# Another order of score, maximum and value-sum work inside a head group of a 32-head attention

## The reference, cut to what matters

```python
def attention_fwd(x, wq, wk, wv, wo, n_heads=32):      # x is layernormed, T=1024, C=512
    xq, xk, xv = (x @ w.T reshaped to [B, T, 32, 16] for w in (wq, wk, wv))
    xq, xk = rotary_pos_emb(xq), rotary_pos_emb(xk)
    scores = einsum('bqhd,bkhd->bhqk', xq, xk) * 16 ** -0.5
    scores = where(causal, scores, -1e30)
    probs = softmax(scores, axis=-1)
    return einsum('bhqk,bkhd->bqhd', probs, xv).reshape(B, T, C) @ wo.T
```

## Time and profile before

| what | value |
| --- | --- |
| runs | 1281.04, 1281.21, 1270.77 us (median 1281.04) |
| profiled execution | 1278.5 us, its span 1276.6 us |
| TensorE busy | 1186.2 us (93%) |
| VectorE busy | 869.9 us (68%) |
| ScalarE busy | 355.9 us (28%) |
| first and last score matmul of the loop (L1582) | 634.6 and 874.7 us |
| scores, x384 | mean of a 512-column one 382 ns |
| exponentials, x384 | mean of a 512-column one 604 ns |

### The profile page before, as it was taken

The page is one execution under the profiler, slowest core; times in us unless marked ns, Lnnn a source line. Parts: engine busy times, 40 slices in busy tenths (PEclk is TensorE's granted clock), DMA queues, the critical chain, the costliest instruction groups (busy, mean ns, idle before and its releaser), DMA issues.

```text
span 1276.6 us, 28155 instructions
## 1 busy us (share of the span) xinstructions
PE 1186.2 (93%) x9962; PEld 513.8 (40%) x9962; DVE 869.9 (68%) x2483; ACT 355.9 (28%) x746; POOL 139.2 (11%) x191
## 2 busy tenths in 40 slices
PE   6799988999999999899899999999979899999992
PEld 3478563433333333444344444433624233333330
DVE  5832675977777773688888888841459677777763
ACT  5434610000000002232176666674110000000010
POOL 2200011111101101352000000000110101111000
PEclk9899978999999999999999999999989999999996
DMA  9100333157724345429405331005751646615556
GB/s 360 46 1 1 153 135 127 51 194 265 266 67 139 112 147 189 165 78 232 90 12 90 57 56 27 2 2 205 318 187 35 256 142 203 202 52 188 187 181 243
DMA packets 63669, 174.33 MB, mean 137 GB/s; under 512 B 9886, under 2 KB 16628, under 8 KB 61352
## 3 DMA queue, kind: packets, MB, share of 16 engines
q1 hardware_dynamic: 55471, 150.60, 36.8%
q0 software_dynamic: 5760, 18.88, 4.3%
q10 hardware_dynamic: 2296, 3.05, 0.7%
HBM read 785.47 MB, written 22.03 MB: 633 GB/s over the span
## 4 chain that ended last, share of the span: by engine, by line
PE 77%; DVE 10%; DMA 4%; ACT 3%; issue 3%; SPq 1%; POOL 1%; POOLq 0%; ACTq 0%; DVEq 0%
PE PS L1096 30%; PE PS L1115 13%; PE PS L1595 6%; PE PS L1582 5%; PE PS L1558 5%; PE PS L817 3%; PE PS L801 2%; PE PS L1622 2%; PE PS L1129 1%; PE PS L1515 1%; PE PS L581 1%; ACT arena L1663 1%; PE PS L565 1%; DVE PS L1716 1%; PE PS L1585 1%
## 5 line engine op out<-in xcount | busy, mean ns | idle before, releaser
L1096 PE MATMUL PS<-arena 128*32 128x400 f32 x3456 | 399.1, 504 | 7.6 <-DMA HH<-in_w 3.7
L1096 PE MATMUL PS<-HH,arena 128*32 128x400 f32 x1152 | 398.5, 504 | 0.0
L1096 PEld LDWEIGHTS PS<-arena 128*32 128x32 f32 x3456 | 144.2, 111 | 256.0 <-issue 248.3
L1286 DVE STREAM_TRANSPOSE arena<-arena 32x192 f32<-32x192 f32 x576 | 211.4, 367 | 7.2
L1716 DVE CUSTOM_DVE_ANT_0 PS<-PS,U 128x128 f32<-128x128 f32 (+7 forms) x256 | 188.0, 783 | 21.3 <-PE PS L1558 20.5
L1115 PE MATMUL PS<-arena 128*32 128x512 f32 x1512 | 195.5, 600 | 4.0 <-DVE arena L1286 4.0
L1663 ACT ACTIVATE arena<-PS 128x512 f32<-128x512 f32 (+3 forms) x384 | 164.2, 495 | 69.2 <-PE PS L1585 48.8
L1264 DVE STREAM_TRANSPOSE arena<-arena 32x128 f32<-32x128 f32 x544 | 164.7, 303 | 16.6 <-DMA arena<-h_scratch,RT 8.7
L1169 ACT ACTIVATE arena<-PS 128x400 f32<-128x400 f32 x72 | 36.2, 503 | 436.5 <-PE PS L1096 436.5
L1270 DVE TENSOR_TENSOR arena<-arena,PS 128x400 f32<-128x400 f32 x72 | 41.0, 572 | 138.1 <-ACT arena L1169 138.1
L1096 PEld LDWEIGHTS PS<-HH,arena 128*32 128x32 f32 x1152 | 126.2, 111 | 0.0
(11 more groups left out here) (255 smaller groups left out, 1250.6 us busy)
## 6 DMA issues: line engine op xcount, KB each, us to landing
arena<-in_w SPq DMA_DIRECT2D x456, 800.0 KB
arena<-in_w2a SPq DMA_DIRECT2D x266, 768.0 KB
HH<-in_w SPq DMA_DIRECT2D x152, 800.0 KB
HH<-in_w2a SPq DMA_DIRECT2D x38, 768.0 KB
arena<-split_scratch SPq DMA_DIRECT2D x96, 128.0 KB, 6.4
arena<-y_scratch SPq DMA_DIRECT2D x24, 256.0 KB, 5.5
split_scratch<-arena SPq DMA_DIRECT2D x8, 768.0 KB, 4.5
arena<-in_w2b SPq DMA_DIRECT2D x72, 64.0 KB
```

The source lines that it names most:

```text
L1096: mm = eng.matmul(PS[SR * j:SR * j + SR, 2 * hf + m, 0:FH], XBT[:, u, c, SR * j:SR * j + SR], W13[j][:, c // 2, m, c % 2, hf * FH:(hf + 1) ...
L1286: tr = eng.transpose(ACT_T[SR * b:SR * b + SR, u, :, rows], src[:, :, SR * b:SR * b + SR])
```

## The change

The string of 98 letters is replaced by another of 98 with the same counts (48 e, 34 m, 12 a, 2 c, 2 t). No instruction, no buffer and no semaphore is added or taken away; the banks of the ring and the counts waited for are worked out from the list as before.

```diff
-        GROUP1 = ("emememeacmeetemeaemememeaemeemeaemeemeacemeteemam"
-                  "meemmemeameemeemmaeeeeammmeeemmemamemeeeamememeea")
+        GROUP1 = ("emememeeemecameeemateemmaememeemeeemacameeteememm"
+                  "aememmeaemeeememeemaaeemeememememmameemeeemaameem")
```

## The result

In 20 runs each the change takes 1268.69 us (median, 1262.45 to 1274.10) against 1276.62 us before (1268.05 to 1282.27). The ratio of the two is 0.9943, with a 95% interval of 0.9927 to 0.9960: 0.6% faster, some 7 us by the ratio (7.9 between the medians), clear of noise and under 1%. A second set of runs on another occasion gave 0.9960 (0.9942 to 0.9978). The forecast was 1273, with 1262 to 1280 as its range, out of a sum of -6.6 us.

The account below looks back on a forecast made before the run. TensorE was taken to bound the loop, with gain in the time it holds no work. Terms of -0.94 us a pass over seven passes gave -6.6 us, 1271.9 from the profiled 1278.5; forecast set at 1273, range 1262 to 1280.

Parts of the forecast that it names:

- wait A: Second turn: TensorE waits 0.36 us for the copy of bank 7; forecast to fall to 0.10, -0.26 a pass.
- wait T: First turn: TensorE waits 0.18 us for a copy; forecast to go, -0.18 us a pass.
- wait B: Fourth score after sum 8: 0.30 us until the first bank is back; forecast to go, -0.30 a pass.
- Step 1: Three pairs of sums (4-5, 8-9, 11-12) save 0.20 us each at their edges, -0.60 us a pass.
- Steps 2 to 4: Both turns and the fourth score after sum 8: wait A -0.26, wait T -0.18, wait B -0.30 us a pass.
- Step 5: Two runs of seven scores: new waits behind ScalarE's pace, 0.15 us each, +0.30 us a pass.
- Step 6: At `mtr`: its slack behind `shift` shrinks from 0.6 to about 0.1 us, +0.10 us a pass.
- Step 7: Pass 7, without maxima: cost of pairs against waits given back, taken as 0, bounds -0.5 and +1.1 us.
- TensorE is full anyway: Loop: waits move rather than go, only 0.35 us a pass to gain, 1276 to 1278 us; chance 0.24.
- All goes: Loop: waits of 0.84 and pairs of 0.69 us a pass all go, none new, 1268 us; chance 0.20.
- VectorE becomes the bound: At `mtr` and the scores behind it: TensorE waits for VectorE, slower than before, 1289 us; chance 0.05.
- The loop's gain does not reach the end: Behind the loop: the weights' traffic sets the end, 1278 to 1281 us; chance 0.03.

Follow-up runs that it names:

- t4_pair89: Kernel before with sum 8 moved behind the second of four masked scores and sum 9 ahead of the third; period 30.50 us against 30.78.
- t6_mtr: Kernel before with `mtr` moved one letter back, behind the first score after sum 9; period 31.22 us against 30.78.
- t2_middle: Kernel before with letters 21 to 50 taken from the change; period 30.31 us against 30.78, loop 235.8 us against 240.0.
- t3_last: Kernel before with letters 51 to 98 taken from the change; period 30.45 us against 30.78, loop 238.4 us against 240.0.
- t8_best: Another string with the change's counts and two pairs of sums, 4-5 and 8-9; period 29.22 us, ratio 0.9910 to the kernel before.
- t5_split: The change with its three pairs of sums taken apart; period 30.64 us against the change's 29.84, ratio 0.9983 to the kernel before.

## Why the prediction was right, term by term

The period fell by 0.94 as forecast, and the loop by 6.6. The mechanism was right: waits A, T and B went, and the pairs saved their edges. That the sum agrees to the hundredth is luck: one term of 0.2 was not seen, and several that came out better than forecast made up for it.

The measured column comes from the distances between the starts of TensorE's matmuls over one period of each kernel, less what the same two kinds of matmul take where nothing is waited for.

| step | forecast | measured |
| --- | --- | --- |
| 1, three pairs | -0.60 | -0.69 (each 0.09 on the way in, 0.12 on the way out, 0.02 in the second sum) |
| 1, not seen: `mtr` loses its neighbour | 0 | +0.21 |
| 2, wait A | -0.26 | -0.32 |
| 3, wait T | -0.18 | -0.15 |
| 4, wait B | -0.30 | -0.30 |
| 5, waits of scores, and of maxima for the ring | +0.30 | +0.29 |
| 6, `mtr` waits for `shift` | +0.10 | +0.03 |
| not placed, each under 0.03 | | -0.01 |
| sum | -0.94 | -0.94 |

- **Step 1** took the price of a sum's edge from the loop's last pair, and the Trainium skill's rule ("TensorEngine Tiling (Array Packing)", Key Properties: changing the tiling mode drains TensorE) for all widths. The rows gave 0.23 a pair and I took 0.20, thinking that a load runs ahead of its matmul; a sum's does so by 0.01 here (709.55 and 709.56), and 0.23 it is. The runs agree with the rule: the price is one of crossing between narrow and full, at every width. Whether the engine drains in that time they do not show. The rule should have been carried further. `mtr` puts its result in 12 partitions, and it behaves as a narrow one: it pays behind a mask and does not beside a sum. Before, it stood beside sum 9 and shared that sum's switches; the earlier trace rows showed both instructions, and I read them for the wait alone. The change moved two scores in between. t4_pair89 and t6_mtr show the 0.2.
- **Steps 2 to 4** were waits read between starts, and each went. Wait T left 0.03: the turn itself starts in time, and its second matmul comes 0.03 later than in the kernel before. Wait A left 0.04.
- **Step 5** was the right size, but the waits lie elsewhere as well. In the change they are 0.12 at score 6, 0.09 at score 31, 0.13 at score 40, 0.08 at score 46, 0.07 at maximum 32 and 0.04 and 0.03 at maxima 14 and 12, together 0.55; before there were 0.26 (0.13 and 0.04 at two scores, 0.06 and 0.03 at two maxima).
- **Step 6**: the slack at `mtr` went from 0.6 to about nothing, as worked out (0.1); the wait is 0.03.
- **Step 7**: pass 7 took 25.7 us before and 25.5 now, from its first score to its last; I had 0. Both sides that I had set against each other are there: in t2_middle it is 24.9 (wait A and the pair 4-5 gone), in t3_last 26.4 (the two other pairs). These 0.2 and the seven passes, which fell by 6.4 and not 6.6 because the first one gained only 0.7, make the 6.6 of the loop.
- **TensorE is full anyway** (0.24) is refuted: the loop's busy share left 0.35 us a pass, and 0.94 was taken out. It read 29.65 of 30 before and reads 30.00 now, with t8_best 0.6 us faster still. Matmul time in a row is no measure of room here.
- **All goes** (0.20) failed on the score runs and on `mtr`'s edge. t8_best, at -1.56 a period, shows that as much (1.53) was to be had, with another string.
- **VectorE becomes the bound** (0.05) did not come. t5_split and t6_mtr show how near it is: 0.2 us a pass each, at the ring. The share that I gave it (88%) divided the busy time of 30 us by a period of 29.8; over one period it is 27.0 of 29.84, 91%.
- **The loop's gain does not reach the end** (0.03) is refuted: the medians fell by 7.9 us and the ratio's interval is 5 to 9, with 6.6 from the loop.
- The time: the sum holds for the difference. The level that I took, 1281, was high by 4 us, since the median of before over 20 runs is 1276.62; the 1.1 us that I added to the sum (1271.9) on its account went in the wrong direction, and 1273 is 4 us above the measured 1268.7.

## What to carry to other kernels

Read room on TensorE from the distances of starts, not from busy time, and sort it by what the next instruction waited for. In a loop that mixes matmuls in a quarter of the columns with full ones, each crossing costs about 0.1 us at the full granted clock of these rows: put the narrow ones side by side, with everything that is narrow counted, transposes into few partitions too. But an engine that feeds on the other kind, with few buffers, runs dry in the meantime, so two sums together paid here, and in the one string with three and another narrow one behind them the gain was lost to waits. And count the waits as well as the crossings: t8_best crosses as often as the change and is 0.62 us a pass faster.

## What the runs showed of the hardware that I had not expected

- A switch between matmuls in 32 (or 12) columns and matmuls in 128 costs 0.09 us on the way in (0.15 from a mask's start to a sum's or to `mtr`'s, against 0.06 to a score's) and 0.12 on the way out (0.55 against 0.43 from the second half of a 512-wide sum to the next). The way out is 0.12 at 128, 256 and 384 columns as well. With the 0.02 in the second sum a pair saves 0.23.
- The loop's time is the same within 0.01 us in two profiles of one kernel (233.41 and 233.42 us), while whole executions of the same kernel differ by up to 14 us. For a change in one stage, one profile told more than twenty runs.
